# Selection of the top 32 and its product with the exponentials: one VectorE instruction, or two on GpSimd

## What is computed

```python
# layer 0, attention (4 heads): only the 32 highest of 77 scores count
scores = einsum('bthd,bghd->bhtg', Q, K) / sqrt(32)
topv, topi = top_k(scores, 32);  probs = softmax(topv)
attn_mean = zeros_like(scores).at[..., topi].set(probs).mean(axis=1)
c_t = einsum('btg,bgd->btd', attn_mean, V)
x = layernorm(x_text) * (1 + gate*scale_in(c_t)) + gate*shift_in(c_t)
y = s4d(x)                      # long convolution, here by DFT
xt = x_text + y * (1 + gate*scale_out(c_t)) + gate*shift_out(c_t)
xt = layernorm(xt + gelu(layernorm(xt) @ W1 + b1) @ W2 + b2)
# then: x += tanh(g) * each of: this, a butterfly FFN, 16-head attention, top-2-of-8 experts
```

## Time and profile before

| | us |
|---|---|
| median of 3 runs | 374.71 |
| lowest, highest | 371.63, 375.29 |
| profiled execution, its own time | 373.9 |
| span in its profile | 372.1 |
| PE busy | 300.9 (81%) |
| DVE busy | 273.7 (74%) |
| ACT busy | 217.8 (59%) |
| GpSimd busy | 112.3 (30%) |

### The profile page before, as it was taken

The page is one execution under the profiler, slowest core; times in us unless marked ns, Lnnn a source line. Parts: engine busy times, 40 slices in busy tenths (PEclk is TensorE's granted clock), DMA queues, the critical chain, the costliest instruction groups (busy, mean ns, idle before and its releaser), DMA issues.

```text
span 372.1 us, 5311 instructions
## 1 busy us (share of the span) xinstructions
PE 300.9 (81%) x1518; PEld 152.2 (41%) x1518; DVE 273.7 (74%) x1214; ACT 217.8 (59%) x453; POOL 112.3 (30%) x174
## 2 busy tenths in 40 slices
PE   2770000599859799979979999999999999999995
...
PEclk9995555689966589999999999999999999999989
...
DMA packets 2624, 9.04 MB, mean 24 GB/s; under 512 B 547, under 2 KB 548, under 8 KB 2340
## 3 DMA queue, kind: packets, MB, share of 16 engines
...
HBM read 7.66 MB, written 1.05 MB: 23 GB/s over the span
## 4 chain that ended last, share of the span: by engine, by line
PE 60%; DVE 31%; ACT 4%; issue 3%; DMA 1%; DVEq 0%
PE bank L457 59%; DVE R L1121 8%; DVE V L1114 6%; DVE MT L1024 5%; DVE arena L1024 4%; ACT arena L776 1%; DVE negm L1028 1%; DVE sel L1054 1%; DVE sm L1058 1%; DMA pack_kgen<-in_kgen 1%; DVE XG L1024 1%; DVE arena L1029 1%; DVE arena L1032 1%; ACT L773 1%; PE bank L538 1%
## 5 line engine op out<-in xcount | busy, mean ns | idle before, releaser
L776 ACT ACTIVATE arena<-bank 128x512 f32<-128x512 f32 (+3 forms) x75 | 38.5, 570 | 34.3 <-PE bank L457 23.2
L773 ACT ACT_TABLE_LOAD x27 | 34.6, 1283 | 28.6 <-PE bank L457 18.7
L457 PE MATMUL bank<-arena 128*32 128x16 f32 (+3 forms) x304 | 12.6, 226 | 41.6 <-DVE arena L1024 41.6
L1121 DVE MATCH_REPLACE8 R<-V,R 128x77 f32<-128x77 f32 x192 | 40.5, 221 | 0.0
L1087 DVE TENSOR_REDUCE pack_bfly<-bank 128x4 f32<-128x308 f32 x64 | 26.1, 468 | 8.9 <-PE bank L457 8.9
L1114 DVE MAX8 V<-R 128x8 f32<-128x77 f32 x192 | 31.2, 223 | 0.0
L457 PE MATMUL bank<-LO,pack_first 128*128 128x512 f32 x48 | 28.1, 678 | 3.1 <-ACT LO L776 2.8
L457 PE MATMUL bank<-arena,pack_dft 128*128 128x256 f32 (+1 forms) x96 | 29.5, 458 | 0.9 <-ACT arena L776 0.7
L457 PEld LDWEIGHTS bank<-arena 128*32 128x32 f32 (+1 forms) x304 | 10.4, 154 | 45.4 <-DVE arena L1024 42.0
L776 ACT ACTIVATE RS<-bank,cst 128x512 f32<-128x512 f32 x24 | 16.5, 688 | 20.3 <-PE bank L457 19.8
L1388 POOL TENSOR_TENSOR k0bd<-sel,w 128x308 f32<-128x308 f32 x16 | 13.3, 828 | 40.2 <-DVE w L1028 39.9
...
## 6 DMA issues: line engine op xcount, KB each, us to landing
...
```

The costliest lines, as they stand in the source:

```text
L457: return nc.tensor.matmul(out, lhsT, rhs, start=start, stop=stop, **kw)
L773: nc.scalar.add_instruction(mybir.InstLoadActFuncSet(name=nc.get_next_instruction_name(), act_func_set_id=need, ins=[], outs=[]))
L776: return nc.scalar.activation(out, in_, func, **kw)
L1121: nc.vector.match_replace(R8[:, g % 2, r % 2, h, :], V8[:, g % 2, h, r, :], src, NEG)\
```

## The change

The selection leaves DVE. GpSimd gets a step `pick` for each of the 16 tiles, with two instructions: the comparison (1.0 or 0.0) into sel, then sel x E0 in place. DVE's part 0 of `weigh` is empty; parts 1 to 3 still wait for `selected`. In round 1 of a tile DVE now waits for the pick of two tiles ago, since that round overwrites `R8[:, g % 2, 1]`. DVE's former wait on `attn_summed` is gone; GpSimd's own order stands for it.

```diff
 def weigh(i, g):
     if i == 0:
-        dve.wait_ge(s["exps_done"], g + 1)
-        dve.wait_ge(s["topk_step"], 32 * (g + 1))
-        if g >= 2:
-            dve.wait_ge(s["attn_summed"], g - 1)
-        nc.vector.scalar_tensor_tensor(sel[:, g % 2, :, :], R8[:, g % 2, 1, :, :], -1.0e38, E0[:, g % 2, :, :],
-                                       ALU.is_le, ALU.mult).then_inc(s["selected"], 1)
+        pass
...
     if tile >= 1:
         weigh(r, g - 1)
+    if r == 1 and g >= 2:
+        dve.wait_ge(s["selected"], g - 1)
...
+elif step.startswith("pick"):
+    pool.wait_ge(s["topk_step"], 32 * (g + 1))
+    pool.wait_ge(s["exps_done"], g + 1)
+    chain(nc.gpsimd.tensor_scalar(sel[:, g % 2, :, :], R8[:, g % 2, 1, :, :], -1.0e38, None, ALU.is_le))
+    tt(sel[:, g % 2, :, :], sel[:, g % 2, :, :], E0[:, g % 2, :, :], ALU.mult).then_inc(s["selected"], 1)
 elif step.startswith("weigh"):
+    pool.wait_ge(s["selected"], g + 1)
     pool.wait_ge(s["weights_ready"], g + 1)
```

All four lists are reordered as well. GpSimd's in full, and the beginnings of the others (without the names that PE ignores, no step is added or dropped):

```diff
 "pool":
-    s_ufly s_coef weigh0/0 weigh1/0 s_qal weigh2/0 weigh3/0 var0/0 var0/1 s_udense mix/0 weigh0/1 s_dfly
-    weigh1/1 weigh2/1 weigh3/1 var0/2 s_dhigh mix/1 s_dlow weigh0/2 weigh1/2 weigh2/2 s_v1 k1/0 weigh3/2 mix/2
-    var0/3 weigh0/3 weigh1/3 weigh2/3 weigh3/3 k1/1 mix/3 k1/2 k1/3
+    s_ufly pick0/0 s_coef pick1/0 weigh0/0 pick2/0 s_qal weigh1/0 pick3/0 weigh2/0 weigh3/0 var0/0 s_udense
+    pick0/1 s_dfly pick1/1 weigh0/1 mix/0 pick2/1 var0/1 weigh1/1 pick3/1 weigh2/1 weigh3/1 s_dhigh pick0/2
+    s_dlow mix/1 pick1/2 s_v1 weigh0/2 pick2/2 weigh1/2 var0/2 pick3/2 weigh2/2 weigh3/2 k1/0 pick0/3 k1/1 mix/2
+    pick1/3 weigh0/3 weigh1/3 var0/3 pick2/3 pick3/3 weigh2/3 weigh3/3 mix/3 k1/2 k1/3
 "dve":
-    s_consts s_kgen0 s_masks s_k0 s_qarg var0/0 s_coef score0/0 score1/0 score2/0 s_w1 s_parg0 var0/1 score3/0
-    s_parg1 weigh3/0 s_qc s_pc0 s_pc1 s_pc2 s_pc3 s_cols s_kern1 s_kern3 film_in/0 score0/1 score1/1 mix/0
-    score2/1 film_pre/0 film_out/0 score3/1 var0/2 weigh3/1 s_bup score0/2 film_in/1 film_pre/1 var1/0 score1/2
-    mix/1 score2/2 var2/0 film_out/1 x1/0 score3/2 var3/0 var1/1 weigh3/2 var0/3 score0/3 film_in/2 fold_down/0
+    s_consts s_kgen0 s_masks s_k0 s_cols s_qarg var0/0 s_coef score0/0 s_parg0 score1/0 s_parg1 score2/0
+    score3/0 s_pc0 var0/1 s_pc1 s_qc s_pc2 weigh3/0 s_pc3 score0/1 film_in/0 s_kern1 s_kern3 s_w1 score1/1 mix/0
+    film_pre/0 score2/1 score3/1 film_out/0 var0/2 s_bup weigh3/1 score0/2 film_in/1 var1/0 film_pre/1 score1/2
+    mix/1 score2/2 var2/0 x1/0 film_out/1 var3/0 score3/2 var1/1 fold_down/0 var0/3 weigh3/2 score0/3 film_in/2
...
 "act":
-    s_kgen0 s_qlag center0/0 var0/0 s_m0 center0/1 s_vw score0/0 var0/1 s_trig score1/0 s_plag score2/0 s_qexp
-    s_qsin s_psin0 s_psin1 s_cols score3/0 vw/0 s_pexp s_psin2 s_psin3 s_kern1 attnT/0 s_kern3 score0/1 s_freq
+    s_kgen0 s_cols s_trig s_qlag center0/0 var0/0 s_m0 s_plag s_vw score0/0 center0/1 s_qexp score1/0 var0/1
+    s_psin0 s_qsin vw/0 score2/0 s_pexp s_psin1 score3/0 s_psin2 s_psin3 attnT/0 s_kern1 score0/1 s_kern3 xt/0
...
 "pe", its own steps from score3/0 to score0/2:
-    score3/0 s_kern0 attnT/0 s_kern1 s_kern2 s_kern3 film_in/0 score0/1 s_freq xt/0 score1/1 dft/0 s_t1
-    center0/2 s_wup score2/1 vw/1 film_pre/0 idft/0 score3/1 center1/0 var0/2 vw/2 center0/3 s_bup score0/2
+    score3/0 score0/1 s_kern0 s_kern1 s_w1 s_kern2 s_kern3 attnT/0 film_in/0 score1/1 xt/0 dft/0 s_freq
+    vw/1 film_pre/0 center0/2 s_t1 vw/2 score2/1 var0/2 score3/1 s_wup s_bup idft/0 center0/3 center1/0 score0/2
...
```

More of the change, by code:

```diff
@@ L94 @@
     "pe": """
[L95 to L114, removed]
@@ L115 @@
-        mixA1/3 mixA2/3 var5/2 moe_out/1 wo/3 logits/2 center5/3 var5/3 units0/2 mix/3 s_psin3 expand/2 units1/2
-        spread0/2 spread1/2 logits/3 moe_out/2 units0/3 expand/3 units1/3 spread0/3 normA/3 spread1/3 s_udense
-        moe_out/3
+        s_k0 weigh0/3 s_cols center0/0 var0/0 x1/0 s_qlag s_m0 score0/0 score1/0 center0/1 weigh1/1 s_vw s_trig vw/0
+        score2/0 weigh2/1 weigh0/0 weigh3/0 var0/1 score3/0 mix/0 s_pc3 score0/1 top2/0 s_psin1 s_kern0 s_kern1 s_w1
+        s_kern2 s_kern3 attnT/0 weigh1/3 film_in/0 score1/1 xt/0 dft/0 s_freq vw/1 x1/1 film_pre/0 center0/2 s_t1
@@ new lines @@
+        vw/2 s_dfly score2/1 var0/2 score3/1 s_wup s_bup s_qal mix/2 s_consts idft/0 center0/3 center1/0 s_parg1
+        score0/2 film_out/0 var1/0 s_kgen0 attnT/1 s_qexp vw/3 film_in/1 film_pre/1 s_masks s_qc xt/1 s_pexp
+        score1/2 dft/1 s_coef ffn_up0/0 s_t2 s_qsin score2/2 ffn_up1/0 center2/0 ffn_down/0 weigh0/1 var2/0 s_wdn
+        weigh2/0 idft/1 film_out/1 center3/0 var3/0 k1/0 center1/1 k1/1 score3/2 var1/1 s_psin0 fold_up0/0
+        fold_up1/0 var0/3 fold_down/0 ffn_up0/1 ffn_up1/1 weigh3/2 center2/1 score0/3 ffn_down/1 attnT/2 center4/0
@@ new lines @@
+        film_in/2 score1/3 var4/0 xt/2 var2/1 weigh3/1 dft/2 s_pc0 k1/2 q/0 center3/1 film_pre/2 var3/1 scoreA0/0
+        score2/3 idft/2 fold_up0/1 film_out/2 fold_up1/1 scoreA1/0 x1/2 weigh3/3 fold_down/1 center1/2 scoreA2/0
+        var1/2 s_v1 scoreA3/0 center4/1 ffn_up0/2 score3/3 ffn_up1/2 top2/3 maxT/0 var4/1 ffn_down/2 keyA0/0 keyA1/0
+        mixA0/0 keyA2/0 attnT/3 mixA1/0 s_ufly film_in/3 mixA2/0 xt/3 var2/2 normA/0 dft/3 wo/0 center5/0 k1/3
+        weigh0/2 q/1 center3/2 var5/0 mix/1 film_pre/3 mix/3 var3/2 top2/1 scoreA0/1 idft/3 scoreA1/1 film_out/3
@@ L131 @@
-        units1/1 maxT/2 expand/1 keyA0/2 keyA1/2 keyA2/2 maxT/3 keyA0/3 normA/2 keyA1/3 keyA2/3 center5/2 normA/3
+        s_kgen0 s_cols s_trig s_qlag center0/0 var0/0 s_m0 s_plag s_vw score0/0 center0/1 s_qexp score1/0 var0/1
+        s_psin0 s_qsin vw/0 score2/0 s_pexp s_psin1 score3/0 s_psin2 s_psin3 attnT/0 s_kern1 score0/1 s_kern3 xt/0
+        dft/0 score1/1 s_freq vw/1 s_t1 film_pre/0 center0/2 vw/2 score2/1 score3/1 var0/2 s_wup center1/0 score0/2
+        attnT/1 var1/0 vw/3 film_pre/1 xt/1 score1/2 dft/1 ffn_up0/0 s_t2 ffn_up1/0 center2/0 var2/0 score2/2
```

29 lines of the change are left out of this document (23 added, 6 removed).

## The result

| | before | after |
|---|---|---|
| median, us | 373.82 (20 runs, 368.75 to 375.47) | 375.64 (20 runs, 373.38 to 378.04) |
| ratio, 95% interval | 1 | 1.0063 (1.0038 to 1.0088) |
| profiled execution, span, us | 373.9, 372.1 | 373.95, 372.2 |
| DVE, GpSimd busy, us | 273.7, 112.3 | 270.2, 145.2 |

The change costs 0.6%, some 2.3 us by ratio, and the interval lies wholly above 1. That is less than the 1% that the prediction took as the least it could tell, and it is on the other side of the forecast of 370.

A forecast was written before the change was run, and what follows sets the result against it. PE waits for DVE until about 162 us, then is itself nearly gapless. Span 372.1 - 4.4 = 367.7, profiled 369.5, plus 0.8 for the median: 370.3, rounded 370 us; 8-in-10 range 363 to 379.

The forecast's parts named there:

- I take s_pc3 at 67.8: Opening on DVE: s_pc3 ends at 67.8 us instead of 71.06, a gain of 3.3 us, and s_kern3 on PE likewise.
- the step on the cover and on GpSimd's queue: Score rounds: 2.0 us of other DVE work hides each undisturbed pick; DVE's wait on `selected` costs nothing.
- The gain of 4.4 us by 162 us: First regime, where PE waits for DVE: everything near 162 us comes 4.4 us earlier, part as fold_up0/0 done ahead.
- the second rival: PE's second clock dip, after the stop at center1/0, goes away: 363 us; chance 0.10.
- The pair at 1.35 us: GpSimd's comparison (0.42 us, at most 0.69) plus product (0.70) and links: a pick takes 1.2 to 1.8 us, taken as 1.35.
- GpSimd's queue could break this.: Long GpSimd steps (s_coef, s_qal, s_dfly, mix) may delay picks; checked through the queue, pick1/1 done near 92, wanted near 98.
- the third rival: Picks stretched to 5.3 us beside DVE's long products, DVE standing 3.3 us: 377 to 383 us; chance 0.17.
- negm's wait, -2.2: Opening on DVE: s_qal now starts after pick2/0 and meets only w, saving 2.2 of negm's 2.97 us wait.
- s_w1 behind s_kern3, selections, Ln, ACT: Opening: s_w1 moved -2.54, selections -1.7, later Ln +1.95 us; ACT's last s_psin near 63.5 instead of 66.43.
- s_freq at 80.7: PE's opening: s_freq may start at 80.7 us instead of 77.52, since score0/1 (5.75) now runs ahead of film_in/0.
- the first rival: PE or ACT was the bound all along, PE perhaps staying at 1.2 GHz: gain absorbed, 374 to 375 us; chance 0.23.
- Nothing after 162 us: Second regime, PE nearly gapless: selections worth nothing; moved steps costed at 0, with 1.5 us either way.

The follow-up runs named there:

- the lists alone: All four new step lists, but the selection stays one instruction on DVE, against the kernel before: 369.4 us, ratio 0.9923.
- batch 0 on DVE: Changed kernel, but batch 0's four tiles are selected by DVE and the other 12 by GpSimd: 373.5 us, ratio 1.0002 to the kernel before.
- no comparison: Changed kernel with each pick only one GpSimd product, E0 x E0: 372.39 us, ratio 0.9964 to the kernel before.
- the filler: Five constant 128x308 matmuls on PE ahead of s_kern0's wait: in the changed kernel 373.1 us, 0.994; in the kernel before 373.83 us, 1.0033.

## Why the prediction was wrong

The step that failed is the opening: "I take s_pc3 at 67.8". It came at 72.98, later than before (71.06). Of these 5.2 us 2.2 are the wait for pick1/0, which the step on the cover and on GpSimd's queue had put at nothing, and 2.6 the stall behind s_qal, which the sum had at 0.8 and which cost w 3.4. The gain of 4.4 us by 162 us was built on that. That the time is only 0.6% up, and inside the 363 to 379 given for 8 in 10, is in part luck: the loss of the opening was given back by a second clock dip that was far shorter, which only the second rival had foreseen.

Starts on PE, in us, each from one traced execution, the fastest of its kernel for the lists alone and without the comparison (the last row is the half-clock time from s_kern0 on up to 140 us, added up from the trace's clock records):

| | before | changed | lists, DVE selects | batch 0 on DVE | no comparison |
|---|---|---|---|---|---|
| s_freq | 77.5 | 90.3 | 87.4 | 86.9 | 87.6 |
| stop before idft/0 | in other order | 2.95 | 1.58 | 3.02 | 2.48 |
| score0/2 | 117.2 | 123.5 | 118.3 | 121.8 | 118.7 |
| idft/2 | 195.0 | 195.6 | 191.4 | 193.9 | 190.8 |
| span | 372.1 | 372.2 | 366.2 | 370.4 | 367.2 |
| clock at 0.5 | 31 | 26 | 23 | 24 | 17 |

Where the opening is alike, single traces repeat well: s_kern0 starts at 69.69, 69.77 and 69.78 in three kernels with batch 0's picks on GpSimd, and at 66.74 and 66.94 in two without.

- **The pair at 1.35 us.** This term was mis-sized: 1.9 undisturbed, because the comparison, scaled from a 512-column row, was 0.98 and not 0.42. Against 2.0 us of cover that alone is still hidden; 12 of 16 picks were never waited for. It costs through the queue: leaving the comparison out gave back 1.0%.
- **"GpSimd's queue could break this."** The step looked at which long step stands ahead of each pick. It didn't add up GpSimd's time in the opening, and it didn't ask what stands behind a pick: mix/0 stands behind pick1/1, and GpSimd's share of it starts at 101.71 instead of 94.85. GpSimd's time is 9.4 to 9.5 us of 10 from 50 to 70, and pick0/0 and s_coef run beside DVE's long s_parg steps, not beside MAX8. Most of s_coef's lateness comes with the lists: it ended at 38.2 before, it ends at 43.5 in the new lists without any pick, and at 44.2 with pick0/0 ahead of it. Without picks DVE doesn't wait for that. The stretch of 30.62 + 1.16 - 28.71 = 3.07 us for pick0/0 was in the third rival (5.3 for a pick), whose place was right and whose price was too high: four waits of 3.8 us in all, the longest 2.2. The Trainium skill (GPSIMD Engine Reference, section 4.1) puts elementwise work on VectorE; these runs agree with it (0.9923 with the selection on DVE, 1.0063 without).
- **negm's wait, -2.2.** Wrong: the stall has no owner. In each trace it falls on the next TENSOR_SCALAR or selection that DVE issues while a half of s_qal runs: negm 3.12 before, w 3.57, sel 2.62, negm 3.40 in four kernels. Maxima, replacements, reductions and reciprocals pass beside it, so it matters which of DVE's instructions comes first. That s_qal would meet w was right; I had 0.8 for it.
- **s_w1 behind s_kern3, selections, Ln, ACT.** With DVE selecting, s_pc3 ends near 70.4, 0.7 ahead of before, where the sum asked for 67.8 (66.6 before rounding up). With the picks it ends 1.9 later. ACT's part was nearly right: s_psin3 ended at 64.2, forecast 63.5.
- **s_freq at 80.7.** The largest miss, 9.6 us: 5.2 of them are s_pc3's lateness (72.98 for 67.8). The other 4.4 have two parts. One is the first rival's mechanism, to which I had given 0.23: PE is at 1.2 GHz until 88.9 us, through film_in/0 and most of dft/0, with gaps of 0.68 and 1.33 us in between, and the filler gave back 1.78 us of it. The other the sum left out: in the new list dft/0 (3.7 us at full clock before, behind s_freq) stands ahead of s_freq, and its second half waits for DVE's reading of s_w1's bank. Moving s_w1 behind s_kern3 was booked as a gain of 2.54 alone. At full clock through dft/0, in the run with GpSimd selecting batch 0 only, s_freq was just 0.48 us earlier. With DVE selecting s_freq is still at 87.4, so most of this comes with the lists.
- **The second dip.** The second rival came true alongside: no half clock between 120 and 133 us. That gives the opening's loss back: fold_up0/0 is 2.2 us ahead of before, of which 0.9 is var0/3, now behind it. I wrote the two rivals as alternatives, and both came: half clock left the one stretch and filled the other, 31 us before and 26 after.
- **Nothing after 162 us.** The lead of 2.2 us is gone at idft/2, which starts 0.6 late: 2.8 us lost, 0.9 of them only var0/3's place. The list run shows this too (fold_up0/0 at 155.1, 7.1 ahead of before; idft/2 only 3.7 ahead), so it is the order and not the picks. PE's waits in between grow from 2.5 to 3.9 us, by one that before has not, in the changed kernel here:

```profile
187.62 0.42 PE L457 MATMUL bank<-pack_first,pack_att 97*128 97x77 f32 x2 [1.64 <-ACT E L776]
```

k1/2 stands there in the new list, k1/1 in the old. No run moved it back.

The account that the runs bear out: the lists bring -0.8%. The picks in batch 0 cost 0.9% (1.0008 against 0.9923), those of the other tiles 0.8% (1.0002 against 0.9923), together 1.4% (1.0063). That this is 0.2 less than the sum is within the intervals. The filler's gain is not a further cost of the picks; it shows what the late clock is worth in this order of steps. What decides the length of the dip behind idft/0 stays open: it was 3.4 us of half clock behind stops of 1.58 and 2.48 us, 6.8 behind 2.95, 10.2 and 13.7 behind 3.02, but also 6.8 behind 2.00 and behind the 1.04 us of the filler's kernel. So a small stop there can cost little or 3 us, and part of the 0.8% of the later picks may be this chance.
